# Making the one-hot rows of the edges' targets for two chunks in one float16 comparison

## The reference

```python
e = leaky_relu(el[src] + er[dst], 0.2)
ex = exp(e - segment_max(e, dst)[dst])
alpha = ex / segment_sum(ex, dst)[dst]
out = segment_sum(alpha[:, :, None] * z[src], dst)
```

## Time and profile before

| | |
|---|---|
| median of 3 runs | 2651.96 us (2649.21 to 2654.1) |
| span of the profiled execution | 2651.4 us |
| PE, DVE, ACT, POOL busy over the span | 95%, 72%, 43%, 5% |
| opening | 0 to about 284.5 us |
| `hot_src` comparisons (line 320) | 196 of 543 ns |
| `hot_dst` comparisons (line 322) | 196 of 251 ns |
| matmuls of the counting loops (line 511) | 588 |

### The profile page before, as it was taken

One profiled execution on the slowest core, in us unless ns is written; L12 is line 12 of the kernel. 1 busy time (PEld: TensorE's weight loads), 2 busy tenths in 40 slices (PEclk: granted clock), 3 DMA queues, 4 the chain that ended last, 5 costly groups with the idle time before them and its releaser, 6 DMA issues. The chain is left out here.

```text
span 2651.4 us, 34230 instructions
## 1 busy us (share of the span) xinstructions
PE 2512.2 (95%) x12453; PEld 1694.3 (64%) x12453; DVE 1914.7 (72%) x2412; ACT 1144.2 (43%) x1344; POOL 128.1 (5%) x151
## 2 busy tenths in 40 slices
PE   6999379969999999999999999999999899998998
PEld 4666268846666666666666666666666566587776
DVE  7876778888987887887798788788878543454111
ACT  5322366565455455555545545555553222121111
POOL 0000000010000000000000000000000000000222
PEclk9999689979999999999999999999999999999999
DMA  5211410053223222222321422222240002025996
GB/s 161 61 33 38 90 58 1 1 169 94 55 53 80 71 62 56 72 60 56 94 55 40 93 63 58 68 71 62 55 118 32 8 12 58 20 63 213 319 334 192
DMA packets 173575, 218.49 MB, mean 82 GB/s; under 512 B 66648, under 2 KB 116442, under 8 KB 173430
## 3 DMA queue, kind: packets, MB, share of 16 engines
q1 hardware_dynamic: 163570, 197.85, 27.3%
q0 software_dynamic: 4928, 10.25, 1.5%
q10 hardware_dynamic: 4932, 8.30, 0.9%
HBM read 187.23 MB, written 32.56 MB: 83 GB/s over the span
## 5 line engine op out<-in xcount | busy, mean ns | idle before, releaser
L1651 PE MATMUL wide_ps<-keep_own_w1g,rails_hid_hi 128*125 128x512 f16 x2120 | 632.5, 380 | 2.9 <-DVE rails_hid_lo L1368 2.9
L1651 PE MATMUL wide_ps<-keep_own_w,rails_hid_hi 128*125 128x512 f16 x2080 | 618.9, 379 | 3.2 <-issue 3.2
L1651 PE MATMUL wide_ps<-keep_own_w1g,rails_hid_lo 128*125 128x512 f16 x1060 | 402.7, 380 | 0.0
L1651 PE MATMUL wide_ps<-keep_own_w,rails_hid_lo 128*125 128x512 f16 x1040 | 394.2, 379 | 0.0
L1651 PEld LDWEIGHTS wide_ps<-keep_own_w1g,rails_hid_hi 128*125 128x125 f16 x2120 | 285.6, 137 | 157.7 <-issue 4.5
L1651 PEld LDWEIGHTS wide_ps<-keep_own_w,rails_hid_hi 128*125 128x125 f16 x2080 | 279.3, 136 | 156.0 <-issue 4.6
L1143 ACT ACTIVATE rails_hid_hi<-rails_raw_a,keep_scale_hidden 128x1000 f16<-128x1000 f32 x210 | 274.2, 1334 | 209.3 <-DVE rails_raw_a L1387 91.9
L1368 DVE SCALAR_TENSOR_TENSOR rails_hid_lo<-rails_raw_a,keep_scale_hidden,rails_hid_hi 128x1000 f16<-128x1000 f32 x210 | 312.1, 1516 | 43.8 <-ACT rails_hid_hi L1143 43.7
L1133 ACT ACTIVATE rails_raw_a<-wide_ps,keep_scale_gelu 128x1000 f32<-128x1000 f32 (+1 forms) x192 | 181.7, 952 | 324.0 <-PE wide_ps L1636 320.9
L1422 DVE SCALAR_TENSOR_TENSOR keep_X<-wide_ps,rails_out_scale,keep_X 125x1024 f32<-125x1024 f32 x180 | 198.6, 1103 | 131.7 <-PE wide_ps L1651 131.6
L1651 PEld LDWEIGHTS wide_ps<-keep_own_w1g,rails_hid_lo 128*125 128x125 f16 x1060 | 145.1, 137 | 84.6 <-issue 0.8
(11 more groups left out here) (414 smaller groups left out, 3543.1 us busy)
## 6 DMA issues: line engine op xcount, KB each, us to landing
carried_w_land<-cproj SPq DMA_DIRECT2D x79, 1024.0 KB
ffn_w<-W SPq DMA_DIRECT2D x51, 1024.0 KB, 13.1
rails_xs<-xt_d SPq DMA_DIRECT2D x124, 78.1 KB
xt_d<-rails_acc SPq DMA_DIRECT2D x20, 250.0 KB, 4.2
keep_X<-x SPq DMA_DIRECT2D x10, 448.0 KB
z_d<-open_z SPq DMA_DIRECT2D x10, 448.0 KB
att_zh<-z_d SPq DMA_DIRECT2D x4, 1120.0 KB
xn_d<-ffn_xn SPq DMA_DIRECT2D x10, 448.0 KB
```

What stands on the lines that cost most here:

```text
L1651: mm = nc.tensor.matmul(ps[0:P, t, :], hid[(q + b) % 2][l][:, k, t * P:(t + 1) * P], w[(q + b) % 2][r][:, k, :], start=(k == 0 and i == 0) ...
```

## The change

The targets' comparison is made once for two neighbouring chunks: a `tensor_tensor` whose first operand is the tile's 125 node numbers, repeated twice, and whose second is the two chunks' target numbers, each repeated 125 times. It needs the target numbers in float16, so they are cast once more (`dst_h`). It comes before the two source comparisons; `hot_ready` now rises at the end of a source comparison. The wait before the first chunk of a pair asks for one used chunk more.

```diff
-        hot_dst = [c.sb(f"hot_dst{k}", [P, P], F16) for k in range(GROUP)]
+        hot_dst = [c.sb(f"hot_dst{k}", [P, 2, P], F16) for k in range(GROUP // 2)]
+        dst_h = c.sb("dst_h", [P, 2 * CHUNKS], F16)
...
                 nc.vector.tensor_copy(src_f[:, 0:CHUNKS], src_i[:])
+                nc.vector.tensor_copy(dst_h[:, 0:CHUNKS], dst_i[:])
...
                 def hots(t):
                     first, groups, done = load_bounds(dve, t)
+                    targets = iota_h[:, t * P:(t + 1) * P].unsqueeze(1)
                     with dve.Fori(0, groups) as g:
                         for k in range(GROUP):
-                            dve.wait_ge(hot_used, done + g * GROUP + (k + 1))
+                            dve.wait_ge(hot_used, done + g * GROUP + (2 if k % 2 == 0 else 1) + k)
+                            if k % 2 == 0:
+                                nc.vector.tensor_tensor(hot_dst[k // 2][:], targets.broadcast_to([P, 2, P]),
+                                                        dst_h[:, bass.ds((first + g) * GROUP + k, 2)].unsqueeze(2).broadcast_to([P, 2, P]),
+                                                        ALU.is_equal)
                             nc.vector.tensor_scalar(hot_src[k][:], iota_h[:], src_f[:, bass.ds((first + g) * GROUP + k, 1)],
-                                                    None, ALU.is_equal)
-                            nc.vector.tensor_scalar(hot_dst[k][:], iota_h[:, t * P:(t + 1) * P],
-                                                    dst_f[:, bass.ds((first + g) * GROUP + k, 1)], None,
-                                                    ALU.is_equal).then_inc(hot_ready, 1)
+                                                    None, ALU.is_equal).then_inc(hot_ready, 1)
...
-                                mm = nc.tensor.matmul(ps_count[:, a:b], hot_dst[k][:], hot_src[k][:, a:b],
+                                mm = nc.tensor.matmul(ps_count[:, a:b], hot_dst[k // 2][:, k % 2, :], hot_src[k][:, a:b],
```

## The result

The change makes the kernel slower by a little over a thousandth: 2655.07 us (median of 20 runs) against 2651.86 us (20 runs of the kernel before), a ratio of 1.0015 with a 95% interval of 1.0008 to 1.0021. Measured again beside two of the experiments it was 2654.68 against 2649.39 us, 1.0017 (1.0008 to 1.0026).

A forecast was written before the change was run, and what follows sets the result against it. The prediction took DVE's pace, and in six loops its restart, to bound the counting loops; 0.9 + 3.1 + 0.5 = +4.5 us on the median 2651.96 gave 2656.5 us, range 2649 to 2663.

The forecast's parts named there:

- What bounds the loops: Counting loops: DVE's pace, 0.617 us a chunk, sets their end; in six loops its restart, 0.96 us after PE's weight load, does too.
- (a) Pace: DVE in the counting loops: a pair of chunks takes 1.247 us instead of 1.235, over 78 pairs +0.9 us.
- (b) Restart: Six loops with buffers filled ahead: DVE waits for PE's second chunk, +0.521 us each, +3.1 us.
- (c) Last chunk: End of nine counting loops: PE enters the last chunk 0.06 us later than before, +0.5 us.
- (d) The handshake: Steady loops: a pair's buffers come back after 2.41 us, DVE wants them after 2.49; cost nothing, thin cover.
- the rival built on it: Buffers come back after 2.6 us instead of 2.41 and hold DVE up: +4.3 us more, 2661 us; chance 0.13.
- (e) First loop: Start-up and first loop: extra cast and later first chunk hidden by 2.2 us of ScalarE cover; cost nothing.
- About 1 us without the cover: Start-up and first loop: what the extra cast and later first chunk would cost if ScalarE hid nothing.
- (f) Odd offsets: PE's weight loads of the second chunk's rows, at odd multiples of 250 bytes: no effect either way.
- Had it packed: Rival: the new comparison takes 0.205 us instead of 0.333, kernel 3.8 us faster, 2648.2 us; chance 0.12.
- No overlap: Rival: the new comparison costs its whole 0.419 us record instead of 0.333, +6.7 us, 2663 us; chance 0.06.
- Nothing arrives: Rival: late restarts are absorbed or PE frees the pair earlier, 2652 to 2653 us; chance 0.09.

The follow-up runs named there:

- e1: The kernel before with only the change's waits, its comparisons left as they were; 1.0013 (1.0004 to 1.0022) of the kernel before's time.
- e3: The kernel before with each target comparison as a 125-element float16 tensor_tensor against one repeated value, waits unchanged; 1.0022 (1.0013 to 1.0031) of the kernel before's time.
- e6: The kernel before with four casts of 1250 numbers added to DVE's start-up; 1.0006 (0.9997 to 1.0015) of the kernel before's time.
- e2: The changed kernel with the pair's first source comparison moved ahead of the pair's wait; 1.0011 (1.0002 to 1.0020) of the kernel before's time.
- e4: The changed kernel with the two chunks' targets interleaved, so the innermost dimension advances in all operands; 0.9979 (0.9970 to 0.9988) of the kernel before's time.
- e5: The changed kernel with interleaved targets and the first source comparison ahead of the pair's wait; 0.9963 (0.9949 to 0.9976), 2641.23 against 2649.39 us before.
- the change again: The changed kernel with nothing altered, run again on another chip; 1.0017 (1.0008 to 1.0026) of the kernel before's time.

## Why the prediction was right, point by point

- **What bounds the loops**, DVE's pace and its restart: right. e1 moved only the restart, e3 only the pace, and each moved the loops it should.
- **(a) Pace**, +0.9 us forecast: the sign was right, the size about half. A pair takes 1.240 us (9.92 us for eight pairs), not 1.247, so 78 x 0.005 = 0.4 us. The form that I took the price from, float32 with a repeated operand, gave 0.333 us; 1.240 - 0.914 leaves 0.326.
- **(b) Restart**, +3.1 us: 1.47 - 0.96 = 0.51 us in six loops, 3.1 us. e1 shows it alone.
- **(c) Last chunk**, +0.5 us: it measured 0.7 us. PE's closing matmul follows the first DVE instruction after the loop by 0.79 to 0.81 us in each of the nine loops, where it was 0.72 or 0.73. No run tries it by itself, but the other traces divide in the same way: 0.71 to 0.74 in e1, e3 and e6, where each chunk has its own target comparison, and 0.79 to 0.84 in e2, e4 and e5, where a pair shares it. What is left of the loops' sum, 4.1 - 0.4 - 3.1 = 0.6 us, agrees.
- **(d) The handshake** does not bind. I had put it at 2.41 us against DVE's 2.49, and for a packed comparison at 2.28 us for four chunks, above DVE's pace. e4 ran four chunks in 2.24 us, DVE's pace, without a wait. My sum of the way back was too long by at least 0.04 us, so the rival built on it had no ground.
- **(e) First loop.** "About 1 us without the cover" was too small: loop 0 ended 2.05 us later (24.10 against 22.05), and the cover was used up:

```profile
15.01 0.42 DVE L324 TENSOR_TENSOR open_hot_dst<-open_iota_h,open_dst_h 125x250 f16<-125x250 f16 x1 [0.87 <-PE open_ps_count L515]
...
17.07 0.42 DVE L324 TENSOR_TENSOR open_hot_dst<-open_iota_h,open_dst_h 125x250 f16<-125x250 f16 x1 [0.72 <-PE open_ps_count L515]
...
24.10 0.28 PE L519 MATMUL open_ps_count<-open_iota_h,open_zeros_h 125*125 125x1 f16 x3
...
24.42 1.21 ACT L595 ACTIVATE open_iota_i<-open_ps_count 125x1250 f32<-125x1250 f32 x1 [0.26 <-PE open_ps_count L519]
```

  (Timeline of the kernel after, start to loop 0's end.) DVE waited twice for a pair while PE was slow at the start, which the kernel before never did (the last section has more on that stretch), and ACT already waited 0.26 us (in the change again it did not wait, and loop 0 ended at 23.95). ACT took the counts no later than before, at 24.42 against 24.55, so nothing arrived, as forecast; but that was luck, since a loop 0 longer by another 0.2 us would have made ACT late.
- **(f) Odd offsets**: weight loads take 136 ns in loops 1 to 9 before and after. Nothing.
- **The rivals.** The comparison did not pack (414 ns, not some 290), as the operand's layout said and not as the 16-bit row did. Had it packed, the nine loops would have been 5.2 us shorter (e4, 106.05 against 111.28), more than the 3.8 us I gave that case, because the handshake did not hold it back. By the whole kernel e4 is 0.21% faster, 5.6 us, with an interval that holds 3.8 us as well. "No overlap" was wrong, 0.326 us for a record of 0.414. "Nothing arrives" was wrong: 3.9 us arrive at the next stage.

The sum, 4.5 us, stands against 4.1 us in the loops, and 0.4 + 3.1 + 0.7 = 4.2 us by its parts. The whole kernel's 3.2 and 5.3 us lie around both and can't test the parts; the traces do.

## What to carry to other kernels

One instruction for two pieces of work also makes one buffer of two and one wait of two. Where an engine restarts from full buffers, the wider wait costs one whole step of the consumer each time (0.51 us here). Put what needs only the first buffer ahead of that wait. And price a merged instruction by its pace with the operand layout it really has: here a repeated innermost operand ate the whole saving, and interleaving the two halves gave it back.

## What was unexpected of the hardware

In loop 0 PE's weight loads of `hot_dst` took 0.23 us instead of 0.14, and matmuls came slowly, until 13.7 us in the kernel before, but until 17.1 us in the kernel after, while the granted clock reads 1.00 in both. The chunks' first weight loads were 1.04 us apart there (14.02, 15.06 and 16.10 us in the kernel after), twice the 0.521 us of the later loops. The windows of 13 to 15 us hold 10 matmuls before and 7 after:

```profile
13.00:15.00 2.00, 2.00 (x10) 1.00 1.02 350
```

```profile
13.00:15.00 2.00, 2.00 (x7) 1.00 1.03 361
```

(The first fence is the kernel before, the second the kernel after; columns: stretch, length, PE busy and matmuls, granted clock, DMA share, GB/s.) Loop 0 took 11.03 us before and 12.94 after; the change again had 12.6 us, e1, e4 and e6 12.3, e2 and e3 12.1 and 12.2, e5 11.0. The slow pace ended at 15.0 us in e5, at 15.8 to 16.3 in e1, e2, e3 and the change again, at 17.0 in e4 and at 19.7 in e6, which also begins the loop 2.9 us later. From the loop's first weight load (12.19 and 12.49 us) it lasted 3.1 us longer after than before; at half the pace that is up to 1.6 us, an estimate from these numbers, of the 1.9 by which loop 0 grew. Since e6, with the waits and comparisons of before, has it too, the change need not be its cause; what sets its end stays open, and in the change it is hidden behind ACT.
